# Shared experts for pairs of tiles with the weights as the stationary operand, and half of the low parts on GpSimd

## The chip, the core and the metric

The kernel runs on one core of a Trainium2 chip. The core has TensorE (PE: matrix products into PSUM), VectorE (DVE), ScalarE (ACT), GpSimd (POOL) and SyncE (SP, which here only starts DMAs); each works through a list of its own in order, and they wait for one another on semaphores. The metric is the time of the program on the device, in microseconds, lower is better.

## What is computed

For 16 sequences ("tiles") of 128 tokens and 512 channels, an RWKV-like mix over time, then a feed-forward layer of shared experts and of 8 routed experts, 2 for each token:

```
x = x + wkv(w, u, layernorm(x), ctx)          # a recurrence over the 128 tokens of a tile
h = layernorm(x)
probs = softmax(h @ gate_w.T); weights, selected = top_k(probs, 2)
moe = sum over the 2 selected experts of weight * (silu(h @ g_e.T) * (h @ u_e.T)) @ d_e.T      # width 256 each
sh  = silu(h @ shared_gate_w.T) * (h @ shared_up_w.T) @ shared_down_w.T                        # width 1024
out = x + moe + sigmoid(h @ shared_expert_gate_w.T) * sh
```

## The kernel before

Precision comes from splitting: each float32 operand of a product is held as a float16 high part and a float16 low part, and three products (high·high, high·low, low·high) stand for one.

**Stages.** The turns `i` = 2 to 15 mix tile i and at the same time compute the shared experts of tile j = i - `LAG`, with `LAG` = 2. Two further sets of shared units (tiles 14 and 15) follow with nothing to mix. Then come 39 slots of 128 gathered tokens, one routed expert each (the expert stage), whose results GpSimd adds into the output by indirect DMAs. All engines' orders are written out by hand, in `turn` for each engine.

**A unit.** The shared experts' 1024 hidden columns are 4 units of 256, u0 to u3. In `products` the tokens (`xt`, 128 by 128) are the stationary operand and the weights (gate 256 | up 256) the moving one: 12 matmuls of 512 columns into `GU` (L884). ACT takes the tanh (`unit_tanh`, L654), DVE makes `hb` in two steps (`hidden`, L1192 and L1195). The result has tokens on the partitions, so `hidden_t` transposes it on PE (2 transposes into the bank `HT`, L829). ACT rounds it to float16 (`unit_hi`, L659), DVE subtracts to get the low part (`hidden_lo`, L1200), and two units later `down_products` makes 6 matmuls of 512 columns into the one bank `DN` (L899). `accumulate` on DVE (L1206) adds a tile's `DN` to x. In a unit PE's order is: 6 of `GU`, the 6 `DN` of two units ago, the `HT` of the unit before, 6 of `GU`.

**The mix of tile i, inside turn i.** `norm` (POOL, three instructions on one column, L411 to L415) and `first_norm` (ACT) give `kb`; PE transposes it (`KT`), DVE subtracts the growth (`keys`), ACT takes the exponentials (`both_exps`, L628, L629), POOL multiplies by the context (`first_product` L421, `second_product` L424), DVE scans over time (`scan_e` L1061, `scan_ev` L1064), adds (`add_now`, L1071) and takes 4 reciprocals; POOL forms the quotient `yb` (`quotient`, L429 and L432). PE transposes `yb` back into `YT` (`y_back`), at the end of the turn. In the next turn DVE adds it to x and takes statistics, POOL and ACT normalise (`second_norm`, L620, gives `xnb`), and PE transposes that into `XT` behind u2.

**The routed experts' weights are made ready beside this**, one expert in two turns. ACT squares them for a scale, POOL computes the scale in ten tiny instructions (`scales`, L467 to L477), ACT makes six pieces (`expert_piece`: high parts L702, scaled copies L705) and POOL subtracts three times (`expert_lo`, L445). So turns alternate on POOL: I call a turn *light* that has one `expert_lo` and ends with `scales`, and *heavy* the next one, which begins with the two list scatters (`scatter`, L488) and has two `expert_lo`. On ACT a light turn ends with two pieces behind the tanh of u3, a heavy one with four. Light turns of the kernel before are 5, 7, ... 15.

## Time and profile before

| | |
|---|---|
| runs of the kernel before | 565.82, 567.20, 568.12 us, median 567.2 |
| the profiled execution | 566.06 us, of which the span from first to last instruction is 564.3 us |
| PE busy | 486.2 us (86%) |
| DVE busy | 421.3 us (75%) |
| POOL busy | 345.4 us (61%) |
| ACT busy | 275.9 us (49%) |
| granted TensorE clock, mean over the span | 0.985 of full |

The span is 1.8 us less than the profiled execution's time. A share of busy time is a mean over stages with different limits; the rows further down read single turns.

### The profile page before, as it was taken

What the parts mean: (1) busy time and instruction counts of PE and PEld (TensorE: products, weight loads), DVE (VectorE), ACT (ScalarE), POOL (GpSimd) and SP (SyncE); (2) the same over time, 40 slices, a digit from 0 to 9 for tenths busy, and PEclk for the clock granted to TensorE, in tenths of its full rate; (3) what the DMA queues carried; (4) which work ended last, traced back from release to release, by engine and by line L of the source; (5) the groups of instructions that cost most, each with busy time, mean ns of one, the idle gap of its engine ahead of it and who ended that gap; (6) DMA issues with size and microseconds to landing.
All of it is one profiled execution on the core that took longest, in us unless ns stands there. A gap on an engine that the chain in (4) does not pass through costs nothing.

```text
span 564.3 us, 10142 instructions
## 1 busy us (share of the span) xinstructions
PE 486.2 (86%) x2671; PEld 258.5 (46%) x2671; DVE 421.3 (75%) x954; ACT 275.9 (49%) x534; POOL 345.4 (61%) x422
## 2 busy tenths in 40 slices
PE   1116789899999999999999979999999999999970
PEld 1113345345455555454555435445545555555530
DVE  5678987899989899999898867566656656666650
ACT  4848837575573864765837333433333333333310
POOL 5767956857948669588486364334375565555332
PEclk9999989999999999999999999999999999999995
DMA  7970105105213223151101320315576776677453
GB/s 283 415 271 19 38 19 187 57 21 188 76 46 143 77 82 143 38 188 62 52 20 39 105 88 15 113 45 102 101 122 117 141 119 116 110 131 123 69 73 38
DMA packets 25929, 59.14 MB, mean 105 GB/s; under 512 B 6314, under 2 KB 6314, under 8 KB 24338
## 3 DMA queue, kind: packets, MB, share of 16 engines
q0 software_dynamic: 9824, 20.90, 21.3%
q1 hardware_dynamic: 16050, 37.59, 18.5%
q8 instruction: 24, 0.39, 0.3%
q14 instruction: 31, 0.25, 0.2%
HBM read 37.83 MB, written 20.65 MB: 104 GB/s over the span
## 4 chain that ended last, share of the span: by engine, by line
PE 52%; POOL 17%; issue 10%; DVE 9%; DMA 7%; ACT 3%; SPq 1%; POOLq 0%; DVEq 0%; ACTq 0%
PE GU L884 28%; PE DN L899 14%; DMA out<-wall,idsa 5%; POOL wall L445 4%; PE XT L829 3%; PE HT L829 3%; POOL yb L429 2%; POOL nrm L411 2%; POOL nrm L413 2%; DVE wall L1071 2%; POOL wall L424 2%; POOL wall L421 2%; DVE wall L1078 1%; PE YT L829 1%; SPq L366 1%
## 5 line engine op out<-in xcount | busy, mean ns | idle before, releaser
L884 PE MATMUL GU<-wall,xt 128*128 128x512 f16 x768 | 187.0, 384 | 2.1 <-DVE wall L1173 2.0
L899 PE MATMUL DN<-wall,hx 128*128 128x512 f16 (+1 forms) x618 | 150.8, 380 | 7.2 <-DVE hx L1200 4.5
L884 PEld LDWEIGHTS GU<-wall,xt 128*128 128x128 f16 x768 | 74.8, 99 | 70.4 <-issue 3.7
L584 POOL DMA_INDIRECT out<-wall,idsa x39 | 62.0, 1590 | 73.1 <-SPq L370 35.1
L659 ACT ACTIVATE hx<-HT 128x256 f16<-128x256 f32 x103 | 39.0, 379 | 127.4 <-PE HT L829 110.6
L899 PEld LDWEIGHTS DN<-wall,hx 128*128 128x128 f16 x618 | 60.4, 98 | 81.9 <-issue 6.0
L1200 DVE TENSOR_TENSOR hx<-HT,hx 128x256 f16<-128x256 f32 x103 | 43.1, 418 | 64.3 <-ACT hx L659 59.7
L654 ACT ACTIVATE th<-GU,scl 128x256 f32<-128x256 f32 x103 | 48.5, 471 | 80.0 <-PE GU L884 76.1
L884 PE MATMUL GU<-wall,kb 128*128 x240 | 61.4, 379 | 0.2 <-DVE kb L1374 0.2
L884 PE MATMUL GU<-wall,xnb 128*128 x228 | 58.5, 379 | 0.6 <-DVE xnb L1374 0.6
L574 POOL DMA_INDIRECT xb<-xn_rows,idsi x39 | 40.2, 1030 | 30.5 <-DMA out<-xb 16.3
L1078 DVE RECIPROCAL wall<-wall 128x128 f32<-128x128 f32 x64 | 57.7, 928 | 0.0
L1192 DVE SCALAR_TENSOR_TENSOR th<-th,GU 128x256 f32<-128x256 f32 x103 | 41.5, 403 | 20.5 <-ACT th L654 20.2
L1195 DVE SCALAR_TENSOR_TENSOR hb<-th,scl,GU 128x256 f32<-128x256 f32 x103 | 49.5, 481 | 9.6 <-DVE th L1192 4.8
L445 POOL TENSOR_TENSOR wall<-wall 128x1024 f16<-128x1024 f32 x21 | 44.9, 2141 | 5.4 <-ACT wall L705 3.5
L488 POOL DMA_INDIRECT lists<-toki,posi x32 | 35.4, 1107 | 13.2 <-issue 6.2
L829 PE MATMUL HT<-ident,hb 128*128 128x128 f32 x206 | 40.1, 276 | 3.3 <-DVE hb L1195 3.2
L411 POOL TENSOR_SCALAR nrm<-mv 128x1 f32<-128x1 f32 x32 | 14.1, 442 | 46.2 <-DVE mv L1086 44.7
L829 PEld LDWEIGHTS HT<-ident,hb 128*128 128x128 f32 x206 | 27.9, 141 | 26.5 <-DVE hb L1195 9.4
L1428 DVE TENSOR_SCALAR wall<-DN,scl,wsl 128x512 f32<-128x512 f32 x39 | 31.3, 802 | 2.9 <-PE DN L899 2.8
L884 PEld LDWEIGHTS GU<-wall,kb 128*128 128x128 f16 x240 | 23.5, 98 | 19.9 <-issue 0.7
L829 PE MATMUL KT<-ident,kb 128*128 128x128 f32 x64 | 11.6, 309 | 23.0 <-POOL toki L395 7.8
(163 smaller groups left out, 747.3 us busy)
## 6 DMA issues: line engine op xcount, KB each, us to landing
wall<-wgu SPq DMA_DIRECT2D x12, 1024.0 KB, 9.7
wall<-wd SPq DMA_DIRECT2D x12, 512.0 KB, 10.3
out<-xb SPq DMA_DIRECT2D x20, 256.0 KB
xb<-x SPq DMA_DIRECT2D x16, 256.0 KB, 2.7
cb<-ctx_t SPq DMA_DIRECT2D x16, 256.0 KB
xn_rows<-xnb SPq DMA_DIRECT2D x16, 256.0 KB
xb<-xn_rows,idsi POOLq DMA_INDIRECT x39
out<-wall,idsa POOLq DMA_INDIRECT x39
```

Source lines behind the costliest of these rows:

```text
L445: ins = nc.gpsimd.tensor_tensor(lo, span(wall, raw, GUW // 2), hi, ALU.subtract)
L574: pool.indirect_dma_start(xg[r], None, xn_dram, bass.IndirectOffsetOnAxis(ap=idsi[:, j:j + 1], axis=0)).then_inc(gather[r], 16)
L584: pool.indirect_dma_start(out, bass.IndirectOffsetOnAxis(ap=idsa[:, j:j + 1], axis=0), ye[j % RESULTS], None, compute_op=ALU.add).then_inc ...
L654: nc.scalar.activation(th[par][:], GU[par][:, 0:IE], ACT.Tanh, scale=scale(row, TANH)).then_inc(tanh, 1)
L659: nc.scalar.activation(hx[par][:, 0:IE], HT[:, 0:IE], ACT.Copy).then_inc(h_hi, 1)
L829: ins = nc.tensor.transpose(dst[:, c * P:(c + 1) * P], src[:, c * P:(c + 1) * P], ident[:])
L884: ins = nc.tensor.matmul(GU[par][:], lhs(xp, c), gate_up(base, wp, c), start=m == 0, stop=m == 3 * HC - 1)
L899: ins = nc.tensor.matmul(DN[:], hx[par][:, hp * IE + c * P:hp * IE + (c + 1) * P], down(base, wp, c), start=start and m == 0, stop=stop an ...
L1078: nc.vector.reciprocal(a, a).then_inc(rcp, 1)
L1192: STT(th[par][:], th[par][:], 1.0, GU[par][:, 0:IE], ALU.add, ALU.mult).then_inc(a1, 1)
L1195: STT(hb[par][:], th[par][:], scale(row, KAPPA), GU[par][:, IE:2 * IE], ALU.mult, ALU.mult).then_inc(h_rdy, 1)
L1200: TT(hx[par][:, IE:2 * IE], HT[:, 0:IE], hx[par][:, 0:IE], ALU.subtract).then_inc(h_lo, 1)
```

## The change

1. **Pairs of tiles.** `shared_products` makes the weights the stationary operand (128 by 128) and the tokens of two tiles the moving one: 24 matmuls of 256 columns for a unit, which is now 128 hidden columns of two tiles. There are 64 units as before. Gate fills columns 0 to 255 of `GU`, up the rest. The hidden values come out with the hidden column on the partition, so the transposes `HT` of the shared units go, ACT's high part and the low part read `th` in SBUF (before: `HT` in PSUM), and `hb` goes. Two banks, `DN0` and `DN1`, hold the two tiles, for 8 units; `accumulate` runs twice every second turn.
2. **Low parts.** `hidden_lo` of u2 and u3 goes from DVE to POOL in the turns: that of u2 stands ahead of `quotient`, that of u3 behind it and ahead of `scales`.
3. **Order.** `LAG` is 3: set 0 of shared units runs beside the mix of tiles 2 and 3, 12 turns (i = 4 to 15) follow, then three sets without a mix. `y_back(i)` moves to the next turn, behind the first 6 matmuls of u0. The front, the last three sets and the weights' pieces are written anew; light turns are now 4, 6, ... 14, heavy ones 5, 7, ... 15. `quotient` writes in place, no longer into `yb`.
4. **Small ones.** `sum_squares` is one matmul, not two (9 times). x has 8 buffers, not 6. The first 6 gathers wait for 14 stored tiles at most, not 16.

```diff
-LAG = 2
+LAG = 3
-NB = 6
+NB = 8
+        def on_pool(n):
+            return SU <= n < N_EXP - 3 * SU and n % SU >= 2
...
             def second_product(t):
+                wait_from(pool, y_t, t - 1)
                 nc.gpsimd.tensor_tensor(wkv(t, 3), wkv(t, 2), part(cb, t), ALU.mult).then_inc(v2, 1)
...
+            def hidden_lo(n):
+                pool.wait_ge(h_hi, n + 1)
+                nc.gpsimd.tensor_tensor(hx[n % 2][:, IE:2 * IE], th[n % 2][:], hx[n % 2][:, 0:IE],
+                                        ALU.subtract).then_inc(pool_lo, 1)
...
                 if i + 1 < B:
                     first_product(i + 1)
                     second_product(i + 1)
+                hidden_lo(SU * j + 2)
                 quotient(i)
+                hidden_lo(SU * j + 3)
                 if sq_e is not None:
                     scales(sq_e + 2, sq_e)
...
             def unit_hi(n, par):
-                act.wait_ge(h_t, n + 1)
+                if n < N_EXP:
+                    act.wait_ge(h_rdy, n + 1)
...
-                nc.scalar.activation(hx[par][:, 0:IE], HT[:, 0:IE], ACT.Copy).then_inc(h_hi, 1)
+                nc.scalar.activation(hx[par][:, 0:IE], th[par][:] if n < N_EXP else HT[:, 0:IE],
+                                     ACT.Copy).then_inc(h_hi, 1)
...
+            def shared_products(n, first, last):
+                u = n % PU
+                for m in range(first, last):
+                    g, c, (xp, wp) = m // (3 * HC), m % (3 * HC) // 3, HI_LO[m % 3]
+                    f = g * IE + u % 2 * P
+                    ins = nc.tensor.matmul(GU[n % 2][:, g * 2 * P:(g + 1) * 2 * P],
+                                           gate_up(sh_base(u // 2), wp, c)[:, f:f + P], xt_pair(n // PU * 2, xp, c),
+                                           start=m % (3 * HC) == 0, stop=m % (3 * HC) == 3 * HC - 1)
+                return ins
...
-                hidden_lo(n + 2, 0)
                 hidden(n + 3, 1, SHARED)
```

**On POOL**, from the last products of a light turn to the head of the next heavy one, before:

```order
L424 TENSOR_TENSOR wall<-wall,cb 128x512
L429 TENSOR_TENSOR yb<-wall 128x512 [waits y_t,rcp]
L432 TENSOR_SCALAR yb<-cb 128x4 [waits ymul]
L467 TENSOR_SCALAR scf<-sci 128x4 [waits exponents]
L468 TENSOR_SCALAR scf<-scf 128x2 [waits scale_step]
```

and now:

```order
L450 TENSOR_TENSOR wall<-wall,cb 128x512 [waits y_t]
L462 TENSOR_TENSOR hx<-th,hx 128x256 [waits h_hi]
L454 TENSOR_TENSOR wall<-wall 128x512 [waits rcp]
L457 TENSOR_SCALAR wall<-cb 128x4 [waits ymul]
L462 TENSOR_TENSOR hx<-th,hx 128x256 [waits h_hi]
L496 TENSOR_SCALAR scf<-sci 128x4 [waits exponents]
L497 TENSOR_SCALAR scf<-scf 128x2 [waits scale_step]
```

Two instructions that wait for ACT's high part (`h_hi`) now stand around the quotient, the second of them ahead of everything that the heavy turn brings.

**On ACT**, at the same place (the end of a light turn and the head of the heavy one), now:

```order
L700 ACTIVATE th<-GU,scl 128x256 [waits h_lo,gu]
L756 ACTIVATE wall<-wall,scl 128x1024 [waits w_hi] x2
L709 ACTIVATE hx<-th 128x256 [waits dn,h_rdy]
L700 ACTIVATE th<-GU,scl 128x256 [waits pool_lo,gu]
L687 ACTIVATE lga<-LG,scl 128x9 [waits logits]
```

The order is that of before; what moved is what the third row waits for (`h_rdy` of DVE, before `h_t` of PE's transpose), and that POOL now waits for it.

**On PE**, u0 of a turn, before:

```order
L884 MATMUL GU<-wall,xt 128x512 [waits h_rdy,sh_d_lo,x_lo]
L884 MATMUL GU<-wall,xt 128x512 x5
L899 MATMUL DN<-wall,hx 128x512 [waits h_lo]
L899 MATMUL DN<-wall,hx 128x512 x5
L829 MATMUL HT<-ident,hb 128x128 [waits h_lo,h_rdy]
L829 MATMUL HT<-ident,hb 128x128
L884 MATMUL GU<-wall,xt 128x512 x6
```

and now, with the transpose of the turn before inside it:

```order
L1012 MATMUL GU<-xt,wall 128x256 [waits h_rdy,x_lo]
L1012 MATMUL GU<-xt,wall 128x256 x5
L919 MATMUL YT<-ident,wall 128x128 [waits x1_rdy,y_rdy]
L919 MATMUL YT<-ident,wall 128x128 x3
L1012 MATMUL GU<-xt,wall 128x256 x6
L1028 MATMUL DN<-wall,hx 128x512 [waits sh_d_lo,pool_lo]
L1028 MATMUL DN<-wall,hx 128x512 x5
L1012 MATMUL GU<-xt,wall 128x256 x12
```

The `HT` rows are gone, and `YT` stands six matmuls of 256 columns behind the end of its turn.

## Rows read from the trace of the kernel before

**Rows 1.** Page: busy time of the engines; the chain that ended last.

```profile
PE 486.2 (86%) x2671; PEld 258.5 (46%) x2671; DVE 421.3 (75%) x954; ACT 275.9 (49%) x534; POOL 345.4 (61%) x422
...
PE 52%; POOL 17%; issue 10%; DVE 9%; DMA 7%; ACT 3%; SPq 1%; POOLq 0%; DVEq 0%; ACTq 0%
```

**Rows 2.** Stages: length, then busy us (instructions) of PE, PEld, DVE, ACT, POOL; clock, DMA.

```profile
44.85:92.66 47.81, 39.08 (x202) 19.14 (x201) 40.82 (x79) 33.65 (x59) 32.78 (x40) 0.96 0.12 39
247.29:266.49 19.20, 18.35 (x107) 9.57 (x107) 18.12 (x44) 10.14 (x22) 17.15 (x24) 1.00 0.38 138
266.49:285.11 18.62, 18.62 (x111) 10.27 (x112) 16.89 (x42) 13.70 (x27) 10.58 (x13) 1.00 0.15 45
322.34:363.63 41.29, 36.35 (x208) 18.48 (x207) 27.00 (x94) 18.27 (x36) 20.95 (x29) 1.00 0.28 92
```

**Rows 3.** PE in order of time (start, us; idle before): the `YT` transposes.

```profile
92.66 0.60 PE L829 MATMUL YT<-ident,yb 128*128 128x128 f32 x4
133.81 0.66 PE L829 MATMUL YT<-ident,yb 128*128 128x128 f32 x4
...
247.29 0.60 PE L829 MATMUL YT<-ident,yb 128*128 128x128 f32 x4
266.49 0.66 PE L829 MATMUL YT<-ident,yb 128*128 128x128 f32 x4 [0.85 <-POOL yb L432]
285.11 0.60 PE L829 MATMUL YT<-ident,yb 128*128 128x128 f32 x4
```

**Rows 4.** PE in order of time: the matmuls of the heavy turn.

```profile
249.03 1.46 PE L899 MATMUL DN<-wall,hx 128*128 128x512 f16 x6
250.32 0.38 PE L829 MATMUL HT<-ident,hb 128*128 128x128 f32 x2
250.54 1.46 PE L884 MATMUL GU<-wall,xt 128*128 128x512 f16 x6
251.84 0.45 PE L856 MATMUL LG<-wr_hl,xt 128*128 128x9 f16 x12
```

**Rows 5.** POOL in order of time: the heavy turn from `scales` to the quotient.

```profile
247.50 0.22 POOL L467 TENSOR_SCALAR scf<-sci 128x4 f32<-128x4 int32 x1 [0.34 <-DVE sci L1150]
...
248.96 1.10 POOL L473 TENSOR_TENSOR scf<-scf 128x1 f32<-128x1 f32 x1
...
251.63 1.12 POOL L477 COPY scl<-sci 128x5 int32<-128x5 int32 x1
...
255.46 2.14 POOL L445 TENSOR_TENSOR wall<-wall 128x1024 f16<-128x1024 f32 x1
...
266.19 0.24 POOL L432 TENSOR_SCALAR yb<-cb 128x4 f32<-128x4 f32 x1
```

**Rows 6.** DVE in order of time: the scans and `add_now` of that turn.

```profile
250.00 1.19 DVE L1064 TENSOR_TENSOR_SCAN wall<-by_time,wall 128x512 f32<-128x512 f32 x1
...
251.50 1.21 DVE L1071 TENSOR_TENSOR wall<-wall 128x1016 f32<-128x1016 f32 x1
```

**Rows 7.** ACT in order of time: the light turn's end, and behind the second norm.

```profile
247.50 0.47 ACT L654 ACTIVATE th<-GU,scl 128x256 f32<-128x256 f32 x1 [0.91 <-PE GU L884]
247.87 2.17 ACT L705 ACTIVATE wall<-wall,scl 128x1024 f32<-128x1024 f32 x2
...
258.97 0.82 ACT L620 ACTIVATE xnb<-xb,nrm 128x512 f32<-128x512 f32 x1 [1.58 <-POOL nrm L415]
```

**Rows 8.** Groups by line (busy us, mean ns; idle before): ACT's high part; PE's stationary loads.

```profile
L659 ACT ACTIVATE hx<-HT 128x256 f16<-128x256 f32 x103 | 39.0, 379 | 127.4 <-PE HT L829 110.6 <-issue 13.6 <-PE DN L899 3.1
...
L884 PEld LDWEIGHTS GU<-wall,xt 128*128 128x128 f16 x768 | 74.8, 99 | 70.4 <-issue 3.7 <-DVE wall L1173 2.5
```

**Rows 9.** PE in order of time: first shared product; last `YT`; first expert product.

```profile
44.85 4.87 PE L884 MATMUL GU<-wall,xt 128*128 128x512 f16 x12
...
322.34 0.60 PE L829 MATMUL YT<-ident,yb 128*128 128x128 f32 x4
...
363.63 0.82 PE L884 MATMUL GU<-wall,kb 128*128 x3 [0.22 <-DVE kb L1374]
```

More of the change, by code:

```diff
@@ L254, in scale, with wait_lo @@
             return span(scl, row * 5 + k, 1)
+        def on_pool(n):
+            return SU <= n < N_EXP - 3 * SU and n % SU >= 2
+        def wait_lo(eng, n):
+            if n >= 0:
+                same = sum(on_pool(k) == on_pool(n) for k in range(n + 1))
+                eng.wait_ge(pool_lo if on_pool(n) else h_lo, same)
         def sh_base(s):
@@ L348, in _ @@
             sp.wait_ge(y_rdy, B)
+            sp.wait_ge(y_t, B - 1)
             load_expert(E - 1)
             store_xn(B - 1)
-            store_sum(B - LAG - 1)
+            store_sum(B - 4)
+            store_sum(B - 3)
             store_probs(1, PART, B)
-            for j in range(B - LAG, B - 1):
-                store_sum(j)
+            store_sum(B - 2)
             store_sum(B - 1)
@@ L542, in turn @@
                     second_product(i + 1)
+                hidden_lo(SU * j + 2)
                 quotient(i)
+                hidden_lo(SU * j + 3)
                 if sq_e is not None:
                     scales(sq_e + 2, sq_e)
-            turns(turn, LAG)
-            expert_lo(E - 2, 1)
-            expert_lo(E - 2, 2)
-            norm(B - 1, 1, agg2, norm2, xn_rdy)
-            scatter(B - 4)
-            for t in range(B - 3, B):
-                scatter(t)
+            turns(turn, LAG + 1)
+            scatter(B - 4)
+            for buf, pattern in ((iotaj, [[1, NSLOT]]), (own_pads, [[0, (NSLOT + 1) // RESULTS], [P, RESULTS]])):
+                link(pool.iota(buf, pattern, base=0, channel_multiplier=0, allow_small_or_imprecise_dtypes=True))
+            assert link.n == CONSTS + LATE_CONSTS
+            norm(B - 1, 1, agg2, norm2, xn_rdy)
+            expert_lo(E - 3, 0)
+            scatter(B - 3)
+            expert_lo(E - 3, 1)
+            expert_lo(E - 3, 2)
+            scales(E, E - 2)
+            scatter(B - 2)
+            scatter(B - 1)
             pool.wait_ge(rt_pos, 1)
@@ L558, in _ @@
                                     bass.IndirectOffsetOnAxis(ap=listi[0:NSLOT, 0:1], axis=0)).then_inc(ids_ld, 16)
+            for k in range(3):
+                expert_lo(E - 2, k)
             scales(E + 1, E - 1)
@@ L765, in turn @@
                         expert_piece(hi_e, k)
-                if hi_e == 0:
-                    expert_piece(0, 4)
-                    expert_piece(0, 5)
-                elif ws_e:
+                if ws_e is not None:
                     expert_piece(ws_e, 4)
                     expert_piece(ws_e, 5)
-            turns(turn, LAG)
+            turns(turn, LAG + 1)
             def gathered_hi(j, r):
@@ new lines, in shared_down @@
+            def shared_down(n):
+                u, pair = n % PU, n // PU
+                wait_lo(pe, n)
+                if pair == 0:
+                    pe.wait_ge(sh_d_lo, u // 2 + 1)
+                for a in range(2):
+                    if u == 0:
+                        wait_from(pe, dn_free, 2 * pair - 1 + a)
+                    for m, (hp, wp) in enumerate(HI_LO):
+                        ins = nc.tensor.matmul(DN[a][:], hx[n % 2][:, hp * IE + a * P:hp * IE + (a + 1) * P],
+                                               down(sh_base(u // 2), wp, u % 2), start=u == 0 and m == 0,
+                                               stop=u == PU - 1 and m == 2)
+                ins.then_inc(dn, 1)
@@ new lines, in shared_units @@
+            def shared_units(j, beside={}, between={}, beyond={}):
+                pe.wait_ge(x_lo, j // 2 * 2 + 2)
+                for u in range(SU):
+                    n = SU * j + u
+                    if n < PU:
+                        pe.wait_ge(sh_gu_lo, n // 2 + 1)
+                    wait_from(pe, h_rdy, n - 1)
+                    shared_products(n, 0, 6)
+                    for step in between.get(u, ()):
+                        step()
+                    shared_products(n, 6, 12)
+                    if n >= 2:
+                        shared_down(n - 2)
+                    for step in beyond.get(u, ()):
+                        step()
+                    shared_products(n, 12, 24).then_inc(gu, 1)
+                    for step in beside.get(u, ()):
+                        step()
@@ L1368, in earlier_adds @@
                 assert wait_step.n == WAIT_STEPS
-            turns(turn, LAG)
+            turns(turn, LAG + 1)
             def gathered_lo(j, r):
```

458 lines of the change are left out of this document (269 added, 189 removed).

## The prediction

> **What bounds the kernel now.** The page's shares come first: PE is busy 86% of the span and makes 52% of the chain that ended last, but POOL makes 17% of it, more than any other engine besides PE [rows 1]. Then the stages: in the turns the clock is full, and of a heavy and the light turn behind it PE is busy 18.35 of 19.20 us and 18.62 of 18.62, DVE 18.12 and 16.89, POOL 17.15 and 10.58 [rows 2]. So the light turn is PE's. The heavy one isn't: PE waits 0.85 us at its end for the quotient [rows 3], and POOL runs from `scales` at 247.50 to the quotient at 266.43 without a wait of note, 18.93 us [rows 5]. The pair takes 285.11 - 247.29 = 37.82 us and is a loop: 19.20 us of POOL from the end of a light turn to the heavy turn's quotient, then 18.62 us of PE. Whatever lengthens POOL's part lengthens the turns.
>
> **The change, on PE.** Six matmuls of 512 columns take 1.29 us (249.03 to 250.32), 215 ns each, of which 512 columns at 2.4 GHz are 213; two `HT` transposes take 0.22 (250.32 to 250.54) [rows 4]. A unit keeps its columns: 24 of 256 cost 24 x (106.7 + 2 to 3) = 2.62 us, where 12 of 512 cost 2.59. Is the stationary load covered? One lasts 99 ns [rows 8], under the 107 ns of a 256-column product, and 12 loads with a 9-column product behind each take 0.45 us with the drain of the last, which is 0.17 in the groups of six (1.46 against 1.29): 24 ns each [rows 4]. So loads overlap one another. I take it as covered; not covered is a rival. A turn then loses 4 x 0.22 of transposes and, if light, about 0.22 with the second sum: 18.62 becomes 17.6, a heavy one 17.35. From the start of `YT` in u0 to the end of a light turn PE needs 16.9 us (17.6 less the 0.65 ahead of it).
>
> **The change, on POOL, and where it hurts.** No row shows a 128x256 subtraction there. The nearest are 128x1024 with float16 output at 2.14 us and a 10-instruction step on one column at about 0.2 us each [rows 5]: 0.19 + (2.14 - 0.19)/4 = 0.68 us; by columns alone 0.53, with the whole fixed part of a short one, 0.8. I take 0.68. Four in a pair are 2.7 us and POOL has 10 us free there. What counts is the place. The low part of u3 waits for ACT's high part, and ACT makes that behind the tanh and the two pieces that end a light turn. Count from the end of PE's light turn (247.29 in the trace of before, call it 0):
>
> - ACT: tanh at 0.21, pieces from 0.58 to 2.75 [rows 7], high part to 3.1 (0.38 us) [rows 8].
> - POOL wants the subtraction at 3.2. DVE's second scan ends at 251.19, that is 3.9 [rows 6], and a POOL instruction of one column that meets a scan takes 1.10 us instead of 0.2 (248.96) [rows 5]. So POOL starts at 3.9 and is done at 4.6. DVE's `add_now` (1.21 us, [rows 6]) had to wait and now holds POOL till 5.7.
> - `scales`: it took 247.50 to 252.75, 5.25 us, of which some 2.6 were such meetings; what is left is 2.5. It ends at 8.2, where it ended at 5.5.
> - the rest is unchanged, 252.75 to 266.43 = 13.7 us [rows 5], plus 0.68 for u2's low part: 22.6.
>
> So the quotient comes at 22.6 instead of 19.1. PE would want it at 17.35 + 0.65 = 18.0. It loses on the way already: `norm` released ACT's `xnb` at 258.97 - 247.29 = 11.7 [rows 7], and now does at 14.4, ACT's 0.8 us makes `xnb` 15.2, and PE reaches `XT` (behind u2) at 12.9 and waits 2.3. ACT's exponentials and the high part of u1 stand behind that norm, which adds about 0.5 at `DN`, and the rest is lost at `YT`. The new loop: 22.7 + 16.9 = **39.6 us for a pair, against 37.8**. Bounds: if the low part slips in ahead of the scan and `scales` meets nothing, 3.2 + 0.5 + 2.6 + 13.7 + 0.5 + 16.9 = 37.4; if `scales` still costs 5.25 behind the 5.7, 42.3. What the change takes from DVE (two subtractions a turn) and what it spares PE in the heavy turn lie beside this loop, and buys nothing in a pair but PE's 1.7 us of the light turn, which the sum has.
>
> A rule of the Trainium skill bears on this. The trace shows the meeting just cited, 1.10 us against 0.2 [rows 5]. The page "SBUF — State Buffer", section "SBUF: two separate sides", says that VectorE instructions with two SBUF inputs and GpSimd instructions take a shared port pair as an exclusive lock for their whole length. By it DVE's own subtraction, which now reads `th` and `hx` in SBUF where it read PSUM, can wait out an `expert_lo` of POOL as well; by the row of before it is only shorter. One such wait a light turn, at most 2.1 us, falls where DVE has that much left and would add nothing.
>
> **The change, by stages** (kernel before in brackets).
>
> - *Front, to the `YT` of turn 5.* Before: first shared product at 44.85 [rows 9], `YT` of tile 3 at 92.66 and of tile 5 at 133.81 [rows 3]. Now the first product needs the second tile too, behind one more norm, `XT` and low part: about 46.4. The mix of tiles 2 and 3 stands beside 4 units, not 8. There DVE is busy 40.8 of 47.8 us [rows 2]; four units less take 4 x 1.2 off, so 36 busy plus 3 of waits: `YT` of tile 3 at 85.3 (82 to 90). Turns 4 and 5 take 21.5 (the last splits of shared weights, 4 us on POOL and 2 on DVE, are in 4) and 18.9 (5 has no `expert_lo`), 40.4 against 41.15: **125.7, 8.1 earlier** (3 to 12).
> - *Turns 6 to 15, five pairs.* Before to 322.34: 188.5. Now four of 39.6 and a last one of 36.0, since turn 15 has no products for a next tile and no first norm (3.6 us off POOL's part): 194.4, so **5.9 more** (-4 to +15).
> - *Behind the last `YT`.* Before 322.34 to 363.63 = 41.29 [rows 9], of which PE is busy 36.35 [rows 2]. Now it is nearly three sets, not two: 3 x 4 x (2.62 + 1.29) = 46.9 less 0.65, plus 1.8 of router, transposes, ranks and sums, 48.1; waits about 2.5, since the last expert's pieces and the first gather come late: 50.6, **9.3 more** (8 to 11). This is the price of `LAG` 3, the front being its other side.
> - *Expert stage.* 363.63 to 564.3: its units don't change, PE sets its pace, the added buffers free the first gathers only. 0 (-1 to +1).
>
> Sum: -8.1 + 5.9 + 9.3 = +7.1 us. On the profiled execution 566.06 + 7.1 = 573.2; the median of the runs is 1.1 us above that execution, so **574.3 us**.
>
> **The rivals.**
>
> - *POOL keeps up, PE sets the pace.* For it: POOL is busy only 27.73 of 37.82 us of a pair [rows 2], and DVE, ACT and PE all get slack. Against it: the order, and the wait for `h_hi` ahead of `scales`. It needs the high part of u3 some 3 us sooner. A pair then is 17.6 + 17.35 + 0.8 us of small waits, near 36, five of them 180 against 194.4: 560 us, 553 with a shorter front.
> - *Few meetings on POOL.* The same loop at its cheap end, 37.6: 8 us less, 566 us, no difference that can be told. A difference under 0.5% (2.8 us) is about what can't be told from no change in this kernel.
> - *More meetings.* The loop at 41.5: 7.6 us more, 582 us.
> - *The stationary load isn't covered by 256 columns.* For it: 99 ns against 107 leaves little [rows 8]. If each product took those 24 ns more, the nine sets in which PE sets the pace (6 light turns, 3 without a mix) would pay 9 x 96 x 24 ns = 21 us: 595 us. The page "TensorE: Matmul & The Clock Gate", section "LDWEIGHTS", states a load of 128 columns at 107 ns, exactly the length of a 256-column product; by it alone the cover would just hold. Against it stand the loads 24 ns apart [rows 4].
>
> **Chances.** The forecast 0.45 (568 to 580), POOL keeps up 0.22, few meetings 0.20, more meetings 0.08, load not covered 0.05. Faster by over 0.5% (under 564.4): the first rival and a little of the second, 0.27. Within: 0.20. Slower: 0.53. The range 556 to 586 leaves out the lowest part of the first rival and the last one.
>
> **What the profile of the changed kernel would show.** Right: in heavy turns PE idle before `XT` about 2 us and before `YT` about 2 us, released by ACT's `xnb` and POOL's quotient; POOL waiting some 2 to 3 us for ACT's `hx` ahead of `scales`; 39 to 40 us from one heavy `YT` to the next; POOL's subtraction near 0.7 us; GU products 109 ns apart; first shared product near 46, first expert product near 371. Wrong: `YT` without idle time, a pair near 36, or products over 120 ns apart. If the front ends at 115 rather than 125, the sum falls by 10 and the sign with it.

## The result, and the profile after

The changed kernel takes 590.3 us (median of 4 runs, 589.22 to 591.61) where the kernel before takes 566.5 on the same chip: 1.042 times as long, with a 95% interval of 1.038 to 1.046. The forecast was 574.3 us with a range of 556 to 586. It was slower, as forecast, but by 23.8 us and not by 7.1, and outside the range. One of the four runs of experiment 5 below took 1323.2 us, more than twice the others, and its median leaves that run out.

The page of the changed kernel shows the same as [rows 1] for before: the busy time of each engine, and the shares of the chain that ended last.

```profile
PE 477.0 (81%) x3293; PEld 316.5 (54%) x3293; DVE 436.3 (74%) x930; ACT 276.5 (47%) x534; POOL 357.7 (61%) x446
...
PE 35%; POOL 16%; DVE 13%; issue 9%; ACT 8%; DMA 6%; SPq 1%; POOLq 0%; ACTq 0%; DVEq 0%
```

PE has 9.2 us less work than before (477.0 against 486.2), as the dropped transposes promise. Yet its share of the chain falls from 52% to 35%, and DVE's rises from 9% to 13%, ACT's from 3% to 8%. PE did not get more work. It got more places at which it waits for the others.

To see where, cut the span at the same five events in both kernels: first shared product, `YT` of tile 5, last `YT` of a turn, first expert product, end. First the two stages of before that [rows 2] does not have (length, then busy us of PE, PEld, DVE, ACT, POOL; clock; DMA):

```profile
44.85:133.81 88.96, 77.22 (x417) 38.48 (x415) 75.49 (x157) 61.51 (x111) 61.79 (x77) 0.98 0.19 63
133.81:322.34 188.53, 184.29 (x1073) 98.25 (x1073) 174.03 (x412) 113.33 (x228) 134.99 (x177) 1.00 0.25 86
```

The same view of the changed kernel:

```profile
47.53:128.14 80.61, 57.99 (x438) 42.78 (x439) 67.28 (x133) 38.61 (x73) 47.84 (x58) 0.87 0.12 37
128.14:329.60 201.46, 179.19 (x1469) 133.59 (x1469) 183.60 (x392) 116.77 (x235) 148.81 (x197) 1.00 0.26 88
329.60:387.69 58.09, 50.31 (x402) 36.58 (x400) 36.31 (x109) 32.65 (x57) 34.72 (x47) 1.00 0.22 68
387.69:587.60 199.91, 180.54 (x944) 97.06 (x944) 113.99 (x240) 56.97 (x118) 94.68 (x72) 0.97 0.57 101
```

Length less PE's busy time is what PE idled. Read side by side:

| stage | before: length, PE busy, idle | after: length, PE busy, idle |
|---|---|---|
| to the first shared product | 44.85 | 47.53 |
| to `YT` of tile 5 | 88.96, 77.2, 11.7 | 80.61, 58.0, 22.6 |
| ten turns, to the last `YT` | 188.53, 184.3, 4.2 | 201.46, 179.2, 22.3 |
| to the first expert product | 41.29, 36.4, 4.9 | 58.09, 50.3, 7.8 |
| expert stage | 200.67 | 199.91 |

The turns got 12.9 us longer though PE has 5.1 us less to do in them: 18.0 us more idling. `LAG` 3 moved 19.2 us of PE's work out of the front, but the front got only 5.7 us shorter in all. Of the moved work 14 us came back behind the turns, where the stage is 16.8 us longer. The expert stage is unchanged.

What PE waited for in the ten turns, from the view of waits (us in total, times, longest):

```profile
PE YT L919 <- POOL wall L457: 10.8, 10, 1.3
PE XT L919 <- ACT xnb L667: 6.8, 5, 1.5
PE DN L1028 <- DVE hx L1330: 1.8, 4, 0.4
PE DN L1028 <- issue: 1.7, 4, 0.4
PE DN L1028 <- DVE xb L1337: 1.3, 1, 1.3
PE LG L966 <- DVE posi L1288: 0.9, 1, 0.9
```

`YT` waits for POOL's quotient in light turns (0.9 us) as in heavy ones (1.3 us). Nine of the ten waits lie in the ten turns, and the tenth (1.0 us) stands just ahead of them, at 128.14. Before, the light turn ended without such a wait [rows 3]. POOL in order of time shows why. This is the end of a light turn and the heavy turn behind it (start us, us; idle before and what ended it). L462 is the low part of `hx`, L496 to L506 are `scales`, L474 is `expert_lo`, L457 ends the quotient:

```profile
225.31 0.67 POOL L462 TENSOR_TENSOR hx<-th,hx 128x256 f16<-128x256 f32 x1 [1.05 <-ACT hx L709]
225.93 1.27 POOL L454 TENSOR_TENSOR wall<-wall 128x512 f32<-128x512 f32 x1
...
229.16 1.06 POOL L462 TENSOR_TENSOR hx<-th,hx 128x256 f16<-128x256 f32 x1 [1.63 <-ACT hx L709]
230.20 1.12 POOL L496 TENSOR_SCALAR scf<-sci 128x4 f32<-128x4 int32 x1
231.40 1.20 POOL L497 TENSOR_SCALAR scf<-scf 128x2 f32<-128x2 f32 x1
...
234.50 0.19 POOL L506 COPY scl<-sci 128x5 int32<-128x5 int32 x1
...
237.65 2.15 POOL L474 TENSOR_TENSOR wall<-wall 128x1024 f16<-128x1024 f32 x1
...
241.08 2.13 POOL L474 TENSOR_TENSOR wall<-wall 128x1024 f16<-128x1024 f32 x1
...
248.95 0.24 POOL L457 TENSOR_SCALAR wall<-cb 128x4 f32<-128x4 f32 x1
```

The low part of u3 waits 1.63 us for ACT and pushes `scales` back, as forecast. But so does the low part of u2: it waits 1.05 us for ACT directly ahead of the quotient (225.93), on which PE's `YT` hangs. The forecast gave that one 0.68 us of work and no wait. In the heavy turn it stands at 246.97 without a wait.

Last, four groups (busy us, mean ns; idle before): PE's 256-column products, DVE's low part from SBUF and from PSUM, POOL's low part.

```profile
L1012 PE MATMUL GU<-xt,wall 128*128 128x256 f16 x1536 | 189.5, 276 | 5.9 <-DVE wall L1304 3.4
...
L1330 DVE TENSOR_TENSOR hx<-th,hx 128x256 f16<-128x256 f32 x40 | 25.4, 635 | 28.8 <-ACT hx L709 28.1
L462 POOL TENSOR_TENSOR hx<-th,hx 128x256 f16<-128x256 f32 x24 | 22.6, 941 | 38.7 <-ACT hx L709 38.7
L1330 DVE TENSOR_TENSOR hx<-YT,hx 128x256 f16<-128x256 f32 x39 | 16.5, 424 | 38.1 <-ACT hx L709 34.0
```

The same subtraction takes DVE 424 ns on average from PSUM and 635 ns when both operands lie in SBUF. Where nothing meets it, the second form takes about 0.4 us too (0.42 at 343.47). The experiments show what the difference is.

### The profile page after: what moved, and what is told of

It is laid out like the page before. It is cut to its first block, busy times and chain, and to the rows that moved or that the text cites. A ratio compares the mean times of both kernels' runs of the same rounds, so it can differ in the third digit from the quotient of the medians.

```text
span 587.6 us, 11209 instructions
## 1 busy us (share of the span) xinstructions
PE 477.0 (81%) x3293; PEld 316.5 (54%) x3293; DVE 436.3 (74%) x930; ACT 276.5 (47%) x534; POOL 357.7 (61%) x446
## 4 chain that ended last, share of the span: by engine, by line
PE 35%; POOL 16%; DVE 13%; issue 9%; ACT 8%; DMA 6%; SPq 1%; POOLq 0%; ACTq 0%; DVEq 0%
PE GU L973 13%; PE GU L1012 7%; PE DN L988 6%; DMA out<-wall,cb 5%; PE DN L1028 4%; POOL wall L474 3%; PE XT L919 2%; DVE hx L1330 2%; PE YT L919 2%; DVE wall L1209 2%; POOL hx L462 2%; DVE pos L1268 2%; ACT wall L675 1%; POOL lists L517 1%; ACT junk L646 1%
## 5 line engine op out<-in xcount | busy, mean ns | idle before, releaser
L1012 PE MATMUL GU<-xt,wall 128*128 128x256 f16 x1536 | 189.5, 276 | 5.9 <-DVE wall L1304 3.4
L1012 PEld LDWEIGHTS GU<-xt,wall 128*128 128x128 f16 x1536 | 150.8, 99 | 37.7 <-issue 3.0
L631 POOL DMA_INDIRECT out<-wall,cb x39 | 62.0, 1589 | 82.9 <-SPq L396 38.7
L1028 PE MATMUL DN<-wall,hx 128*128 128x512 f16 x384 | 93.9, 381 | 13.0 <-DVE hx L1330 5.5
L988 PE MATMUL DN<-wall,hx 128*128 x234 | 56.9, 379 | 1.0 <-DVE hx L1330 1.0
L1325 DVE SCALAR_TENSOR_TENSOR th<-th,scl,GU 128x256 f32<-128x256 f32 x103 | 49.5, 480 | 9.3 <-DVE th L1323 4.1
L474 POOL TENSOR_TENSOR wall<-wall 128x1024 f16<-128x1024 f32 x21 | 44.9, 2142 | 10.8 <-ACT wall L756 10.7
L621 POOL DMA_INDIRECT xb<-xn_rows,cb x39 | 38.6, 989 | 17.1 <-issue 8.8
L1330 DVE TENSOR_TENSOR hx<-th,hx 128x256 f16<-128x256 f32 x40 | 25.4, 635 | 28.8 <-ACT hx L709 28.1
L462 POOL TENSOR_TENSOR hx<-th,hx 128x256 f16<-128x256 f32 x24 | 22.6, 941 | 38.7 <-ACT hx L709 38.7
L709 ACT ACTIVATE hx<-th 128x256 f16<-128x256 f32 x64 | 26.1, 408 | 33.2 <-DVE th L1325 33.0
L988 PEld LDWEIGHTS DN<-wall,hx 128*128 128x128 f16 x234 | 22.9, 98 | 28.6 <-issue 1.5
```

The costliest lines, as they stand in the source:

```text
L474: ins = nc.gpsimd.tensor_tensor(lo, span(wall, raw, GUW // 2), hi, ALU.subtract)
L631: pool.indirect_dma_start(out, bass.IndirectOffsetOnAxis(ap=idsa[:, j:j + 1], axis=0), ye[j % RESULTS], None, compute_op=ALU.add).then_inc ...
L709: nc.scalar.activation(hx[par][:, 0:IE], th[par][:] if n < N_EXP else HT[:, 0:IE], ACT.Copy).then_inc(h_hi, 1)
L988: ins = nc.tensor.matmul(DN[j % 2][:], hx[par][:, hp * IE + c * P:hp * IE + (c + 1) * P], down(base, wp, c), start=m == 0, stop=m == 3 * I ...
L1012: ins = nc.tensor.matmul(GU[n % 2][:, g * 2 * P:(g + 1) * 2 * P], gate_up(sh_base(u // 2), wp, c)[:, f:f + P], xt_pair(n // PU * 2, xp, c) ...
L1028: ins = nc.tensor.matmul(DN[a][:], hx[n % 2][:, hp * IE + a * P:hp * IE + (a + 1) * P], down(sh_base(u // 2), wp, u % 2), start=u == 0 and ...
```

## The experiments

Times are medians; the kernel before took 565.6 to 566.1 us beside them. A *pair* is a heavy and a light turn: 37.8 us before, 40.4 in the changed kernel. The first theory was that of the prediction: POOL's chain sets the pair, and the low parts stand in it at bad places.

### 1. All low parts on DVE

The second part of the change undone: `hidden_lo` of u2 and u3 goes from POOL's program back to DVE's, that of u3 behind the second scan as in the kernel before.

```
             def on_pool(n):
-                return SU <= n < N_EXP - 3 * SU and n % SU >= 2
+                return False
...
# POOL's turn
-                hidden_lo(SU * j + 2)
                 quotient(i)
-                hidden_lo(SU * j + 3)
...
# DVE's turn
                 scan_ev(i)
-                if j == 1:
-                    hidden_lo(n - 1, 1)
+                hidden_lo(n - 1, 1)
...
+                hidden_lo(n + 2, 0)
                 hidden(n + 3, 1, SHARED)
```

> The changed kernel with all four low parts of a turn on VectorE again, the last one behind the second scan as in the kernel before; GpSimd makes none. Theory A (GpSimd's chain sets the pair of turns, and the two low parts stand in it): with them gone the chain is that of before, 19.2 us from the end of a light turn to the heavy turn's quotient, and PE's light turn is 17.6, so the pair falls from 40.4 to 36.5 to 37.5 us and the whole to 571 to 577 us. Rival B (the low parts on GpSimd are innocent, and VectorE, which now reads two SBUF operands and meets GpSimd, or the 256-column products, make the turns long): the pair stays over 39.5 us and the whole over 585. Under both, the stretch behind the last YT stays at 58 us, since no low part there is GpSimd's.

Measured: 589.9 us (1.042, interval 1.040 to 1.044), the same as the changed kernel; the pair 40.4 to 40.9 us. Theory A, which was mine, failed with its numbers, and rival B's bounds hold. Moving the work from POOL to DVE bought nothing, so another chain stood right behind POOL's. The heavy turn of this kernel, all engines in order of time, shows it:

```profile
237.01 2.68 DVE L1328 TENSOR_TENSOR hx<-th,hx 128x256 f16<-128x256 f32 x1
237.26 2.14 POOL L474 TENSOR_TENSOR wall<-wall 128x1024 f16<-128x1024 f32 x1
...
239.62 0.94 DVE L1207 RECIPROCAL wall<-wall 128x128 f32<-128x128 f32 x1
...
240.48 1.30 DVE L1335 SCALAR_TENSOR_TENSOR xb<-DN,gate,xb 128x512 f32<-128x512 f32 x2
...
241.27 2.72 PE L1026 MATMUL DN<-wall,hx 128*128 128x512 f16 x6 [2.73 <-DVE xb L1335]
```

A subtraction of 0.4 us stands for 2.68 us on DVE, to 239.69, and POOL's `expert_lo` ends at 239.40. Its record begins 0.25 us ahead of POOL's, beside the end of a scatter (236.27 to 237.24), so the start times alone do not say which of the two was first. Behind it stand a reciprocal and the two accumulates (L1335), and PE waits 2.73 us for them. That last wait is the change's too: a pair of tiles now shares the two `DN` banks, and both must be emptied between the last `DN` product of one pair and the first of the next, one unit of products apart. Before, the one bank `DN` had to be emptied within one unit of products as well, but by one `accumulate`; now two stand there.

The wait has a second price in this turn. The granted clock from 241.27 to 243.78 was 0.50, and the six `DN` products took 2.51 us from the first to what follows them, where 1.29 is usual. It was so behind the waits of 2.73 and 3.03 us and for a part of the products behind that of 3.14, and not behind those of 2.72 and 2.74. PE's busy time in the ten turns is 181.5 us in this run and 179.6 in the next.

### 2. The same with POOL's long instructions in pieces

```
-                ins = nc.gpsimd.tensor_tensor(lo, span(wall, raw, GUW // 2), hi, ALU.subtract)
+                for q in range(4):
+                    w = GUW // 2 // 4
+                    ins = nc.gpsimd.tensor_tensor(lo[:, q * w:(q + 1) * w], span(wall, raw + q * w, w),
+                                                  hi[:, q * w:(q + 1) * w], ALU.subtract)
```

> The kernel of the first experiment (all low parts on VectorE, 589.9 us, pair 40.4 to 40.9) with every expert subtraction of GpSimd issued in four pieces of 256 columns. It tells why VectorE couldn't take the low parts. Theory A (a GpSimd instruction shuts VectorE's instructions on two SBUF operands out until it ends: the low part of u0 took 2.68 us beside one of 1024 columns, and the accumulate behind it came late for DN, 2.7 us): the longest low part falls under 1 us, the wait of DN for the accumulate from 2.7 to about 1, the pair by 1 to 2 us in spite of nine more GpSimd instructions, and the whole to 580 to 586 us. Rival B (VectorE is simply full, and nobody shuts it out): the low part of u0 stays over 2 us, and the whole within 1% of 589.9 or above it.

Measured: 579.9 us (1.025, 1.020 to 1.030), 10 us less than experiment 1 with the same work in more instructions. The group of DVE's low parts in experiment 1 and here:

```profile
L1328 DVE TENSOR_TENSOR hx<-th,hx 128x256 f16<-128x256 f32 x64 | 47.6, 744 | 27.1 <-ACT hx L707 27.0
```

```profile
L1331 DVE TENSOR_TENSOR hx<-th,hx 128x256 f16<-128x256 f32 x64 | 34.3, 535 | 29.7 <-ACT hx L710 28.1 <-DVE cb L1465 0.8 <-issue 0.6
```

In the pair from 205.7 to 244.3 us PE now waits 0.5 us for the accumulates, where it was 2.73, and the ten turns go from 202.3 to 195.6 us, of which 1.9 are PE's own busy time. The pair is 2.0 us shorter and the whole just under theory A's range; the longest low part in the pair, 1.36 us, did not fall under 1. So theory A of this run holds in its mechanism: DVE was not only full, it was shut out while a POOL instruction ran, and the length of that instruction was the price. What PE waits for most in this pair is POOL's quotient again, 1.57 us at the heavy `YT`: the two chains are nearly equally long.

This is the rule that the prediction cited from the Trainium skill, page "SBUF — State Buffer", section "SBUF: two separate sides": the pair of ports is held for the full instruction, and the loser is blocked. The traces agree that DVE gets on only when POOL's instruction ends, 2.68 us beside 2.14.

### 3. The same test behind the turns

In the stretch behind the last turn of the changed kernel DVE and POOL, in order of time:

```profile
345.59 2.04 DVE L1264 TENSOR_SCALAR sci<-scw 128x2 int32<-128x2 int32 x1
347.54 0.15 DVE L1267 TENSOR_TENSOR counts<-counts,LG 128x8 f32<-128x8 f32 x1
347.62 2.10 DVE L1268 TENSOR_TENSOR pos<-ones,pos 128x16 f32<-128x16 f32 x1
...
371.98 2.17 DVE L1330 TENSOR_TENSOR hx<-th,hx 128x256 f16<-128x256 f32 x1 [2.84 <-ACT hx L709]
```

```profile
345.48 4.21 POOL L474 TENSOR_TENSOR wall<-wall 128x1024 f16<-128x1024 f32 x2 [2.89 <-ACT wall L756]
...
369.65 6.49 POOL L474 TENSOR_TENSOR wall<-wall 128x1024 f16<-128x1024 f32 x3 [7.78 <-ACT wall L756]
```

An instruction on two columns takes 2.04 us, and one on 16 columns 2.10; one beside them that reads `LG` in PSUM takes 0.15. PE's waits at `DN` follow:

```profile
350.51 1.47 PE L1028 MATMUL DN<-wall,hx 128*128 128x512 f16 x6 [0.87 <-DVE hx L1330]
...
360.30 1.46 PE L1028 MATMUL DN<-wall,hx 128*128 128x512 f16 x6 [1.57 <-DVE xb L1337]
...
374.21 1.47 PE L1028 MATMUL DN<-wall,hx 128*128 128x512 f16 x6 [1.87 <-DVE hx L1330]
```

The edit cuts only the six `expert_lo` behind the last turn into four pieces each (the loop of experiment 2, with `parts=4` at those calls).

> The changed kernel, in which the six subtractions of expert weights that GpSimd makes behind the last turn are issued in four pieces of 256 columns each, instead of one of 1024. Theory A (in this stretch VectorE's small instructions stand for as long as a GpSimd instruction runs: 2.04, 2.10 and 2.17 us, just the 2.1 of one subtraction of 1024 columns): the longest small VectorE instruction falls to under 1 us, and PE's waits for DN and KT in the stretch (0.87, 1.87, 0.64 us) fall by 2 to 3 us together: 587 to 588.5 us in all. Rival B (those lengths have another cause): they stay near 2 us, and the stretch stays at 58 us or gets longer with GpSimd's added instructions: 590 to 592 us.

Measured: 588.1 us (1.039, 1.037 to 1.041), and the stretch is 56.11 us long, 2.0 less:

```profile
331.98:388.09 56.11, 50.30 (x402) 36.52 (x400) 32.23 (x109) 32.61 (x58) 35.87 (x64) 1.00 0.19 61
```

DVE's busy time in it falls from 36.3 to 32.2 us, with no instruction fewer: 4.1 us were time shut out. From 340 us on no DVE instruction takes over 1 us. The waits of 0.87 and 0.64 us are gone and that of 1.87 is 0.21. That for the accumulates is 1.92 instead of 1.57, since what stands ahead of it on DVE is as long as before, and one for `hx` of 1.33 us is new just ahead of the gather; both took back part of it. The time alone would not show the gain: the intervals of this kernel and of the changed one overlap, and in the profiled execution the front ended 2.4 us later than in the changed kernel's (130.50 against 128.14), with a granted clock of 0.83 against 0.95 from 86 to 111 us, so that the spans are 587.7 and 587.6 us. What shows it is the stretch itself.

### 4. POOL's order alone

```
-                hidden_lo(SU * j + 2)
                 quotient(i)
-                hidden_lo(SU * j + 3)
+                hidden_lo(SU * j + 2)
                 if sq_e is not None:
                     scales(sq_e + 2, sq_e)
+                hidden_lo(SU * j + 3)
```

> The changed kernel with GpSimd's order alone changed: the quotient ahead of the low part of u2, and the scales ahead of the low part of u3. Nothing is left out. Theory A (the place costs, not the work): the light turn's YT no longer waits 0.9 us for the quotient, and the scales begin some 2.7 us sooner in the heavy turn, so the second norm, XT and the quotient come sooner: the pair falls from 40.4 to 36.5 to 38 us, the whole to 571 to 579 us. Rival B (the work and its meetings with VectorE cost, wherever they stand; or u2's low part comes late for its DN product behind YT): the pair stays over 39 us, the whole over 583.

Measured: 581.2 us (1.028, 1.024 to 1.031), pair 38.2 us. Nothing was removed, and 9 us went: the place of two short instructions cost that. Pair and whole came just outside theory A's ranges and clear of rival B's, and PE still idled 2.3 us in the pair (view of waits):

```profile
PE YT L919 <- POOL wall L457: 0.7, 1, 0.7
PE DN L1028 <- POOL hx L462: 0.7, 1, 0.7
...
PE DN L1028 <- DVE hx L1330: 0.4, 1, 0.4
...
PE XT L919 <- ACT xnb L667: 0.4, 1, 0.4
```

### 5. The low parts in place, but one column wide

```
-                nc.gpsimd.tensor_tensor(hx[n % 2][:, IE:2 * IE], th[n % 2][:], hx[n % 2][:, 0:IE],
+                nc.gpsimd.tensor_tensor(hx[n % 2][:, IE:IE + 1], th[n % 2][:, 0:1], hx[n % 2][:, 0:1],
```

> The changed kernel, in which GpSimd's two low parts of a turn subtract one column instead of 256, in their places and with their waits: 255 columns of these low parts are left out. If the waits and places cost (A), only the 0.47 us of 255 columns goes, four times a pair and some of it beside other waits: the pair falls by 0.5 to 1.9 us, the whole by 2 to 10 us (580 to 588). If the length of the subtraction and the meetings that it brings cost (B), the pair falls by 3 us or more and the whole to under 576.

Measured: 581.3 us (1.028, 1.025 to 1.030), pair 39.1 us, that is 1.25 us less. The pair is in theory A's range, and the whole at its lower end. So the length of the subtractions costs too, but with the work nearly gone the pair is still 1.3 us longer than before, and 0.9 us longer than with all the work at better places (38.2, experiment 4). Both take from the same waits, so 1.25 and 2.2 us need not add up.

### 6. More of POOL's order, then the stretch behind the turns, then the front

Three kernels, each on top of the one before, starting from experiment 4. First POOL's turn:

```
-                scatter(i - 4)
                 pool.wait_ge(nd, i + 1)
...
-                if lo_e is not None:
-                    expert_lo(lo_e, 1)
                 norm(i - 1, 1, agg2, norm2, xn_rdy)
+                if lo_e is not None:
+                    expert_lo(lo_e, 1)
...
                     first_product(i + 1)
+                if lo_e is not None:
+                    quotient(i)
+                if i + 1 < B:
                     second_product(i + 1)
+                if lo_e is None:
+                    quotient(i)
                 hidden_lo(SU * j + 2)
+                scatter(i - 3)
                 hidden_lo(SU * j + 3)
                 if sq_e is not None:
                     scales(sq_e + 2, sq_e)
```

> On from the kernel with GpSimd's order changed (581.2 us, pair 38.2, in which PE still waits 2.4 us and GpSimd's heavy turn has 21 us without a wait). Further changes of GpSimd's order alone: the second norm ahead of the first expert subtraction, in heavy turns the quotient ahead of the next tile's second product, and the scatters between the two low parts at a turn's end instead of at its start, so that the scales come behind the scans. Nothing is left out. Theory A (GpSimd's chain is still what keeps PE from its own pace of 35.8 us a pair): PE's waits fall to under 1 us, the pair to 36 to 37 us, the whole to 570 to 575 us. Rival B (VectorE or ACT are the next bound right behind): the pair stays over 37.5 and the whole over 577 us.

Measured: 567.1 us (1.004, 1.001 to 1.007), 14.1 us less than experiment 4, pair 36.2 to 36.9 us, and the whole better than theory A's range. In the ten turns PE is busy 177.20 of 183.08 us:

```profile
126.94:310.02 183.08, 177.20 (x1471) 133.51 (x1469) 174.91 (x394) 116.73 (x236) 144.53 (x198) 1.00 0.28 98
```

Against the changed kernel's 201.46 that is 18.4 us for order alone, with every instruction still there.

Second, behind the last turn: `expert_lo` in four pieces, `accumulate(B - 4)` and `accumulate(B - 3)` ahead of `rows_of_lists()` on DVE (the wait of 1.57 us in experiment 3), and the two iotas behind the second norm on POOL.

> The same kernel with three changes behind the last turn: expert subtractions in four pieces, the two accumulates ahead of the rows of the lists on VectorE, the two iotas of GpSimd behind the second norm. Theory A (of the 58.1 us of this stretch PE needs 50, and the rest is waits that these three places make): the stretch falls to 52 to 55 us, and the time lies 3 to 6 us under the kernel without them. Rival B (what is won is given back at the first gathered rows, which the expert stage waits for): within 1.5 us of it.

Measured: 566.6 us (1.002, 1.000 to 1.004). The stretch goes from 55.98 to 53.55 us, as theory A has it, but only 0.5 us of it shows in the medians, which is rival B's bound: the times of the two kernels do not settle whether it reached the end. In the profiled execution the first 62 us were 1.3 us longer than in the kernel without the edit; 36 products from 51 us on took PE 5.32 us there and 4.51 in the other, though the edit lies behind the turns.

Third, DVE ahead of turn 4:

```
                 residual_and_stats(2)
-            hidden(2, 0, SHARED)
             shared_gu_lo(2)
-            reciprocals(3, 0, 2)
-            hidden_lo(2, 0)
+            hidden(2, 0, SHARED)
             keys(4)
             first_stats(5)
+            hidden_lo(2, 0)
+            reciprocals(3, 0, 2)
+            reciprocals(3, 2, 2)
             hidden(3, 1, SHARED)
-            reciprocals(3, 2, 2)
             act_lo(2)
```

> The same with a fourth change, VectorE's order ahead of turn 4: the split of shared weights 2, the keys of tile 4 and the statistics of tile 5 move into the 2.6 us in which VectorE waited for a tanh, and all reciprocals of tile 3 come ahead of hidden(3). Theory A (in the front PE idles 22.6 us for a chain of VectorE, ACT and GpSimd and not for work of its own, so order decides): the YT of tile 3 comes at 79 to 82 us instead of 85, and 3 to 5 us of that reach the end. Rival B (what comes sooner waits in turns 4 and 5, whose splits of shared weights bound them): YT of turn 5 comes at 126 to 128 as before, and the time stays within 1.5 us.

Measured: 561.7 us, ratio 0.9946 with an interval of 0.992 to 0.997: faster than both kernels, and 28.6 us under the changed kernel. `YT` of tile 3 comes at 81.7 us, where it came at 85.1, as theory A has it, and the median falls by 4.9 us. Not all of that need be this edit's. Against the first kernel of this experiment, whose trace has no such delay at its start, the front ends 3.8 us earlier (123.16 against 126.94), the stretch behind the turns is 2.5 us shorter and the expert stage 0.8 longer; that is 5.5 us in the spans and 5.4 in the medians. So front and stretch together reach the end. The stages of the kernel:

```profile
47.50:123.16 75.66, 58.13 (x438) 43.07 (x439) 65.55 (x133) 37.64 (x72) 48.58 (x58) 0.89 0.12 39
123.16:306.24 183.08, 177.20 (x1471) 133.54 (x1469) 174.91 (x394) 116.74 (x236) 144.58 (x198) 1.00 0.29 98
306.24:359.70 53.46, 49.93 (x403) 36.67 (x401) 32.04 (x109) 33.54 (x58) 35.48 (x64) 1.00 0.18 62
```

PE still idles 17.5 us in the front, against 5.9 in the turns and 3.5 behind them. That is the largest reserve in the stages that the change touches; the expert stage idles 19.4.

### 7. What each part of the change is worth by then

The kernel of 561.7 us with all low parts on DVE (the edit of experiment 1), and all of POOL's expert subtractions in pieces so that DVE isn't shut out long:

> The best kernel so far (GpSimd's new order, drain and front, 561.7 us, pair 36.9) with all low parts on VectorE again and every expert subtraction of GpSimd in four pieces. It tells whether the second part of the change (low parts on GpSimd) is worth anything once the order and the length of GpSimd's instructions are right. Theory A (VectorE, with 175 us of 183 busy in the turns, has no room for two low parts more, and a pair's two accumulates stand right before DN): the pair gets longer by 0.6 to 1.6 us and the whole comes to 565 to 570 us, so GpSimd's low parts are worth 3 to 8 us. Rival B (the lock and the order were all, and the place of the low parts doesn't matter): 560 to 563 us.

Measured: 566.7 us (1.002, 1.000 to 1.004). Turns and the stretch behind them:

```profile
122.92:309.09 186.17, 178.35 (x1471) 133.23 (x1469) 177.13 (x413) 117.84 (x236) 137.56 (x223) 1.00 0.28 96
309.09:364.60 55.51, 50.39 (x402) 36.42 (x401) 32.82 (x110) 33.52 (x58) 34.57 (x63) 1.00 0.18 60
```

So the kernel with low parts on POOL behind the quotient is some 5 us ahead of the one with all of them on DVE. The two differ in the pieces of `expert_lo` in the turns as well, and no run has these with the low parts on POOL, so the 5 us are what both make together.

And the kernel before with the same three changes of POOL's order in its turns, to see how much any kernel would have had from them:

> The kernel before, one tile at a time and with its transposes, with the same three changes of GpSimd's order in its turns: second norm ahead of the expert subtraction, in heavy turns the quotient ahead of the next tile's second product, the scatters at a turn's end ahead of the scales. It tells how much of what the order gives is the change's and how much any kernel would have had. Theory A (in the kernel before only 0.85 us of a heavy turn is a wait for the quotient, so order can give at most that, five to six times): 561 to 564 us, and pairs of 37.0 us. Rival B (VectorE, with 18.12 of 19.20 us busy in a heavy turn, is next): within 1.5 us of 566.

Measured: 564.4 us (0.996, 0.995 to 0.998), and a pair of 37.6 us: 1.4 us less. That lies between both ranges and decides little between them. It does decide the question it was made for. The three changes of order that give the changed kernel 14.1 us (581.2 to 567.1, behind the 9 of experiment 4) give the kernel before 1.4.

```profile
132.07:319.92 187.85, 184.86 (x1073) 97.71 (x1073) 172.37 (x412) 113.27 (x228) 128.38 (x178) 1.00 0.26 86
```

Its PE is busy 184.86 of 187.85 us there. It has 7.7 us more work in the ten turns than the changed kernel in good order. That is what the change had to give in the turns. The edits behind the turns and in the front were not tried on the kernel before, so 561.7 against 564.4 us is not what the change alone is worth; no run shows that. By the stages `LAG` 3 gives nothing: in the kernel of 561.7 us the front ends 10.7 us earlier than before (123.16 against 133.81), and the stretch behind the turns is 12.2 us longer (53.46 against 41.29).

## Why the prediction was right or wrong

Its sum was -8.1 + 5.9 + 9.3 + 0 = +7.1 us. Measured in the traces: -5.7 + 12.9 + 16.8 - 0.8, which unrounded is +23.3 (587.6 against 564.3). Of the 16.2 us that the sum missed, 7.5 are the stretch behind the turns, 4.0 the last pair, 3.1 the four pairs before it and 2.4 the front, less 0.8 of the expert stage. The steps that failed are the first two: in the stretch the sum put 2.5 us of waits where 7.8 came, and in the last pair it put POOL's wait for ACT's `hx`, 2.46 us, at nothing.

- *The products of 256 columns* were right. 24 of them take 2.62 us from start to start in a full stretch (216.02 to 218.64), 109 ns each, as forecast; the load is covered, and that rival is out. PE's own pace is near what the rival "POOL keeps up" said: 36.9 us a pair in experiment 6, against 36.
- *POOL's subtraction* at 0.68 us was right where it meets nothing (0.67 at 225.31). On average it took 0.94, since it meets DVE.
- *Its place in the heavy turn* was the right mechanism with a fair size. PE waited 1.33 at `XT` and 1.33 at `YT` (forecast: about 2 each), released by ACT's `xnb` and POOL's quotient as it said, and 1.63 was POOL's wait ahead of `scales` (2 to 3). Experiment 4 confirms the place of the two low parts as the cause.
- *The term that was too small in the pair* is the meetings of `scales` with DVE. The sum counts from the end of the light turn's products, which before is the start of `YT`; now `YT` stands six products behind it. The changed kernel's PE and ACT there:

```profile
224.56 2.13 PE L1012 MATMUL GU<-xt,wall 128*128 128x256 f16 x18
226.07 0.47 ACT L700 ACTIVATE th<-GU,scl 128x256 f32<-128x256 f32 x1 [0.84 <-PE GU L1012]
227.59 0.66 PE L919 MATMUL YT<-ident,wall 128*128 128x128 f32 x4 [0.90 <-POOL wall L457]
```

  Twelve of the 18 products belong to the light turn, so it ends at 225.87, and the tanh comes 0.20 behind, where the forecast had 0.21. The low part of u3 is done at 4.3 us from there (4.6 forecast). Then the first instruction of `scales` meets DVE's second scan and the second one meets `add_now`, 1.12 and 1.20 us for them. So DVE holds POOL until 6.7 us and not until 5.7, and `scales` ends at 8.8 and not at 8.2. The heavy `YT` comes at 23.4 (22.7). From a heavy `YT` to the end of the light turn's products PE took 17.0 us (208.88 to 225.87), and 16.9 was forecast. Together that is 40.4 instead of 39.6.
- *The wait of 0.9 us at the light turn's `YT`* was not forecast: the sum gave u2's low part its work and not its wait for ACT. By the trace it costs the pair nothing by itself, since POOL's chain from `scales` to the heavy quotient does not wait for PE, and PE waits for it at `XT` and `YT` anyway. Experiment 4 agrees: there the light `YT` has no wait, PE's part is 17.1 us as before, and what got shorter is POOL's, from 23.4 to 21.1.
- *The last pair* was forecast at 36.0 and took 40.0. The reasoning took 3.6 us off POOL, since turn 15 has no next tile. But a POOL with less to do only waits longer for `hx`, 2.46 us there, and the quotient stands behind that:

```profile
326.91 0.67 POOL L462 TENSOR_TENSOR hx<-th,hx 128x256 f16<-128x256 f32 x1 [2.46 <-ACT hx L709]
```

  Work taken from an engine that waits for another engine's result is no gain.
- *DVE's lock* was named and given away. The prediction cited the rule, saw that the low part now reads two SBUF operands, and concluded that one such wait "would add nothing". It adds nothing as long as POOL is the later engine; experiments 1 and 2 show 10 us behind it, ready to take over from POOL, and experiment 3 shows 2 us of it in the changed kernel behind the turns. What it costs that kernel inside the turns no run shows. So the sentence that VectorE's relief was worth nothing was right for the wrong reason: DVE's busy time in the ten turns rose from 174.0 to 183.6 us, with 20 instructions fewer.
- *The front* was forecast to end 8.1 us earlier, and ended 5.7 earlier. `YT` of tile 3 was right (85.1 against 85.3); turn 4 took 22.4 us against 21.5, and turn 5 20.6 against 18.9. Turn 5 is a heavy one without `expert_lo`; POOL waited in it 1.57 us for ACT's exponentials and 1.05 us for ACT's `hx` ahead of the quotient, which the sum did not have.
- *Behind the last turn* was the worst term: 58.1 against 50.6. PE's busy time there was 50.3 instead of 48.1, probably since the small products and the end of a matmul ahead of each wait were counted too low. The waits were 7.8 instead of 2.5. Experiment 3 shows 2 us of them as DVE shut out by `expert_lo`, and the second kernel of experiment 6, against the first, shows 2.4 us for the three places together; POOL's new order in the turns had taken 2.1 before. The forecast had allowed waits for the last expert's pieces and the gather only.
- *The range* treated each unknown by itself. It had a case for more meetings on POOL (582 us), but none in which `scales`, the last pair and the stretch behind go wrong together. They did, because all three rest on the same assumption, that an engine is late only by its own work.

## What to carry to other kernels

A short instruction that waits for another engine costs its queue the wait and not its length, so put it behind whatever the bounding engine wants next; here two subtractions of 0.7 us at the wrong place cost 9 us. Where VectorE and GpSimd both work on SBUF, count the longest instruction of the one as a possible delay of any short one of the other, and cut the long one. When a change relieves one engine and the time doesn't fall, undo that part or take its work away, look for the chain behind it, and only then judge the idea.

## What the runs showed of the hardware

- A DVE instruction on 2 columns took 2.04 us beside a POOL subtraction of 1024 columns, and one on 16 columns 2.10, where both take about 0.15 to 0.17 alone; one that reads PSUM took 0.15 in between. One on 256 columns took 2.17 beside the same kind. So the price there was the rest of POOL's instruction, whatever the size of DVE's. The first of them has a single SBUF operand, which I had not expected.
- Cutting POOL's subtraction into four pieces costs POOL little (35.9 us busy in the stretch behind the turns, 34.7 uncut) and gave DVE 4.1 of 36.3 us back there.
- A stationary load of 99 ns under a product of 256 columns is hidden: 109 ns from product to product.
- In the kernel of experiment 1 PE's waits of 2.73 and 3.03 us for DVE were followed by six 512-column products in 2.5 us instead of 1.29, at a granted clock of 0.50.
- In the front, where PE waits up to 9 us at a time, the granted clock was 0.87 of full speed (0.98 before), which is time at the lower of its two levels. The 256-column products there took 2.51 us for 12 (62.10 to 64.61 in experiment 4), against 1.30 at full clock, so PE pays for its idling a second time.
